# Two transfers instead of one: the spread of the attention's maxima over 125 partitions

## The reference, cut to what matters

```python
scores = jnp.einsum('bhtd,bhsd->bhts', Q, K) * scale
scores = jnp.where(mask, scores, jnp.float32(-jnp.inf))
attn = jax.nn.softmax(scores, axis=-1)
out = jnp.einsum('bhts,bhsd->bhtd', attn, V)
out = out.transpose(0, 2, 1, 3).reshape(B, Tt, D)
out = out @ Wo.T
return hidden_states + jnp.tanh(gate) * out
```

## Time and profile before

| | us |
|---|---|
| median of 3 runs | 1405.7 |
| lowest and highest run | 1401.32, 1408.68 |
| the profiled execution, whole | 1402.65 |
| its span, first to last instruction | 1400.8 |
| PE busy | 1331.3 |
| DVE busy | 928.5 |
| ACT busy | 734.7 |
| POOL busy | 489.8 |

### The profile page before, as it was taken

The page is one execution under the profiler, slowest core; times in us unless marked ns, Lnnn a source line. Parts: engine busy times, 40 slices in busy tenths (PEclk is TensorE's granted clock), DMA queues, the critical chain, the costliest instruction groups (busy, mean ns, idle before and its releaser), DMA issues.

```text
span 1400.8 us, 42823 instructions
## 1 busy us (share of the span) xinstructions
PE 1331.3 (95%) x17120; PEld 937.6 (67%) x17120; DVE 928.5 (66%) x2431; ACT 734.7 (52%) x1772; POOL 489.8 (35%) x550
## 2 busy tenths in 40 slices
PE   6999999999999999897899999999999999999977
PEld 5777777777777777666566666766676667666624
DVE  3555555555555555547677877787888888887862
ACT  4776677767667667632425453445345434444332
POOL 3222111222222222113346445543555345534540
PEclk9999999999999999988999999999999999999979
DMA  7333222222222223113000010001010110010000
GB/s 228 99 106 106 93 75 63 74 73 71 61 76 74 75 69 101 54 57 122 22 21 14 23 28 21 15 22 28 22 27 9 28 27 22 10 26 22 15 14 14
DMA packets 39529, 73.70 MB, mean 53 GB/s; under 512 B 17797, under 2 KB 20485, under 8 KB 37829
## 3 DMA queue, kind: packets, MB, share of 16 engines
q1 hardware_dynamic: 39365, 71.24, 17.2%
HBM read 60.24 MB, written 7.57 MB: 48 GB/s over the span
## 4 chain that ended last, share of the span: by engine, by line
PE 82%; DVE 8%; issue 6%; DMA 2%; ACT 1%; SPq 1%; POOL 0%; DVEq 0%; ACTq 0%; POOLq 0%
PE b_bank L1831 18%; PE b_bank L1837 12%; PE ring_bank L703 7%; PE ring_bank L704 6%; PE ring_bank L705 6%; PE av_bank L789 4%; PE b_bank L1945 4%; PE score_banks L762 4%; DVE probs L450 3%; PE b_bank L1982 3%; PE score_banks L749 3%; PE b_bank L1971 2%; PE b_bank L1885 2%; DVE probsT L467 2%; PE av_bank L775 2%
## 5 line engine op out<-in xcount | busy, mean ns | idle before, releaser
L1126 POOL TENSOR_TENSOR rst<-rp,st 128x448 f32<-128x448 f32 x192 | 209.7, 1115 | 55.9 <-DVE st L1349 53.9
L450 DVE CUSTOM_DVE_ANT_0 probs<-score_banks,unmask 112x375 f32<-112x375 f32 x256 | 124.8, 544 | 93.0 <-issue 93.0
L595 ACT ACTIVATE probs<-probs,least_inv 112x375 f32<-112x375 f32 x256 | 152.4, 606 | 32.5 <-DVE least_inv L450 32.5
L467 DVE SCALAR_TENSOR_TENSOR probsT<-score_banks,least_cols 125x448 f32<-125x448 f32 x192 | 107.9, 617 | 53.9 <-PE score_banks L762 51.7
L610 ACT ACTIVATE probsT<-probsT,key_mask 125x448 f32<-125x448 f32 x192 | 114.5, 661 | 47.4 <-DVE probsT L467 47.2
L1118 POOL TENSOR_TENSOR xm<-mixed,xa 128x448 f32<-128x448 f32 x80 | 88.0, 1102 | 145.3 <-DVE mixed L1278 140.0
L340 POOL TENSOR_TENSOR aT_lo<-whole,aT_hi 128x375 fp32r<-128x375 f32 x64 | 59.0, 921 | 152.3 <-ACT whole L576 150.2
L375 POOL TENSOR_TENSOR ctx_rstd<-ctx_var_eps,a_eps_exp 125x3 f32<-125x3 f32 x16 | 13.8, 865 | 272.6 <-DVE ctx_var_eps L423 272.6
L703 PE MATMUL ring_bank<-aT_hi,wk_lo 128*128 128x376 f32 x256 | 91.2, 356 | 0.2 <-issue 0.2
L1628 ACT COPY key<-b_bank 128x448 f32<-128x448 f32 x16 | 8.5, 533 | 148.4 <-PE b_bank L1831 148.4
L704 PE MATMUL ring_bank<-aT_lo,wk_hi 128*128 128x376 f32 x256 | 85.5, 334 | 0.0
(11 more groups left out here) (183 smaller groups left out, 3109.0 us busy)
## 6 DMA issues: line engine op xcount, KB each, us to landing
least_cols<-values_of_two_batches SPq DMA_DIRECT2D x32, 437.5 KB
ctx_tok<-in_ctx SPq DMA_DIRECT2D x16, 672.0 KB
xT_sb<-in_xT SPq DMA_DIRECT2D x16, 224.0 KB, 2.9
inv_cols<-values_of_two_batches SPq DMA_DIRECT2D x128, 28.0 KB, 3.9
x_tok<-in_x SPq DMA_DIRECT2D x16, 224.0 KB, 2.7
x_between_layers<-x_tok SPq DMA_DIRECT2D x16, 224.0 KB, 4.7
b_x<-x_between_layers SPq DMA_DIRECT2D x16, 224.0 KB, 3.0
x_post<-x_between_layers SPq DMA_DIRECT2D x16, 224.0 KB, 2.9
```

Source lines behind the costliest of these rows:

```text
L450: dve.tensor_tensor_reduce(out=probs[:, g % 2, i], in0=score_bank[0:T, i, 0:TC], in1=unmask[:, m[1]], scale=-SCALE, scalar=-LOWEST, op0=AL ...
L467: dve.scalar_tensor_tensor(out=probsT[:, g % 2, k].rearrange("p (i t) -> p i t", t=T), in0=score_bank[0:TK, :, k * T:(k + 1) * T], scalar= ...
L595: act.activation(probs[:, g % 2, i], probs[:, g % 2, i], ACT.Exp, scale=-1.0, bias=least_at(m, g, i), accum_out=sums[:, g, i:i + 1]).then_ ...
L1126: pool.tensor_tensor(by_chunk(rst[:, j % NPROD]), by_chunk(rp[:].rearrange("p c t -> p (c t)")), state_of(j), ALU.mult).then_inc(s_pprod, 1)
```

## The change

The one transfer onto 125 partitions is issued as two, onto partitions 0 to 111 and 112 to 124, each with the same two source rows. Both count on the same semaphore, so the wait asks for 32 where it asked for 16. The order of everything else stays.

```diff
-            sp.dma_start(least_cols[:, 2 * half:2 * half + 2],
-                         rows_in_dram(half, 0).rearrange("(o g) f -> o g f", o=1).broadcast_to([TK, 2, HG * T])).then_inc(s_least_in[half], 16)
+            for part in CTX_PARTS:
+                sp.dma_start(least_cols[part, 2 * half:2 * half + 2],
+                             rows_in_dram(half, 0).rearrange("(o g) f -> o g f", o=1).broadcast_to(
+                                 [part.stop - part.start, 2, HG * T])).then_inc(s_least_in[half], 16)
...
-                dve.wait_ge(s_least_in[g // 2], 16 * count(m, 1, 1))
+                dve.wait_ge(s_least_in[g // 2], 32 * count(m, 1, 1))
```

## The result

| | before | after |
|---|---|---|
| median of 21 runs, us | 1405.03 | 1398.78 |
| lowest run, us | 1399.84 | 1396.83 |
| the profiled execution, us | 1402.65 | 1402.71 |

The ratio of the runs is 0.9965, with a 95% interval from 0.9955 to 0.9975: 4.9 us less (3.5 to 6.3), within 0.5%. Both profiled spans are 1400.8 us. That is not a contradiction: the execution profiled after is the slowest of its 21, and the one before is among the faster of its own. So the two traces must be compared stretch by stretch and not by their ends.

The account below looks back on a forecast made before the run. PE was taken to bound the kernel, busy 1331.3 of 1400.8 us; only the last step's 1.2 us wait would go, with nothing from the loop, giving 1404.5 us off a median of 1405.7; range 1399.5 to 1409.0.

Parts of the forecast that it names:

- The transfer uses about five engines: Spread of the maxima: 125 partitions use about 5 of 16 engines, 112 would use 16; 2.2 of 3.2 us go.
- landing of 3.7 us: Split transfer of the maxima: lands 3.7 us after its first issue instead of 5.56, bounds 2.7 and 6.9 us.
- The second issue: SP's queue: the split's second transfer costs one more step of SP, 0.3 us with the gap behind it.
- Nothing is gained in the loop: Attention's loop: transfers already have 2.8 to 10.6 us of slack, so a batch stays at 36.4 us.
- SP's extra issues are covered: SP: 32 more issues, 9.6 us in all, covered by its 297.3 us of standing in front of line 266.
- The whole stall goes: Last step, half 1: DVE's whole wait of 1.21 us for the maxima goes, for any landing under 4.4 us.
- PE takes the gain: Last step: of PE's 1.97 us idle, 1.21 go and pass through fully to the store; 0.76 us of idling stay.
- A: Rival, last step: the clock stays up behind the shorter idle time, 1.6 us more, -2.8 us, 1402.9 us; chance 0.17.
- D: Rival, loop: lighter DMA traffic also removes PE's gaps, 4.6 us, 5.8 with the last step, 1399.9 us; chance 0.07.
- B: Rival, the split transfer: 112 partitions spread no better, the wait grows by 0.3 to 1.3 us, 1406.0 to 1407.0; chance 0.10.
- C: Rival, second layer: the moved timing brings lower-clock stretches of 1.6 us each, slower; chance 0.06.
- the sign that the prediction set for it: Profile after: the prediction is wrong if stretches at the lower clock come or go by more than two.

Follow-up runs that it names:

- e3: Against the kernel before, the maxima's transfer stays one but goes onto 128 partitions instead of 125; ratio 0.9978, median 1399.55 us.
- the two filled: The kernel before with 14 or 7 matmuls added in PE's idle time of the last step, slow transfer kept; ratios 1.0017 and 0.9999.
- e1: Against the kernel before, only the attention's last spread (last batch, half 1) is split, the other 31 stay one transfer; ratio 0.9980, median 1399.49 us.
- f1: The changed kernel, unedited, run again beside fresh runs of the kernel before; ratio 0.9982, median 1400.05 us.
- g2: The changed kernel, unedited, run a third time against the kernel before; ratio 0.9987, median 1402.48 us.
- f2: The kernel before, unchanged, run as if it were a changed one against itself; ratio 1.0021, median 1404.49 us.

## Why the prediction was right, point by point

- **The transfer uses about five engines, and the 112 partitions would spread over all.** Shown: in the same half microsecond the share went from 0.49 to 0.95 and the rate from 149 to 351 GB/s. A landing of 3.7 us was forecast for the split; it has no landing row. The single transfer of e3 has 3.7, but by the prediction's own terms it should have had 5.56 - 2.2 = 3.4, without the second issue. So the same number is partly luck: the spread saved 1.9 us, not 2.2. The second issue was sized at 0.3 us and costs SP 0.49 (0.76 us for two, 0.27 for one), which stayed hidden too. The rule of the Trainium skill on how many engines carry a transfer ("DMA: Bandwidth & Descriptors", "Why a DMA increments its semaphore by 16 and not by 1") holds here for 125, 112 and 128 partitions. Its rule against splitting ("Rules for kernel authors") is given for two halves that each spread over all 16 engines already; the 125 partitions did not, and there the split gained. e3 fits its advice to use one transfer of 128.
- **Nothing is gained in the loop, and SP's extra issues are covered.** Shown: 36.40 us a batch as before, and 543.1 us over 30 spreads with and without the split.
- **The whole stall goes, and PE takes the gain.** Shown: the wait has no row, and DVE's use comes 6.40 us after the write of line 266 instead of 7.69, 1.3 us sooner for the 1.2 forecast. In other executions of the kernel before the same wait was 1.4 to 1.8 us, so 1.21 us was the low end of that term.
- **The clock was held to be a rival, A, with a chance of 0.17.** This is where the size was off: the forecast of 1.2 us puts nothing down for the clock. What A describes was in fact a part of the gain in this pair of traces: in three of the five unfilled executions with the unmoved stall the clock fell behind PE's gap, in none of the six without the wait and in neither of the two filled. That a shorter gap keeps the clock up rests on these counts; what makes it fall in one execution and not in the next stays open. The mean step of those five is (22.23 + 22.60 + 20.81 + 22.74 + 20.79) / 5 = 21.8 us; without the wait it is 19.3. So 2.5 us are to be had in that step, of which 1.5 are the stall and 1.0 the clock's mean share, an estimate from only five executions.
- **The size by the runs.** Five comparisons remove the wait and change nothing else of weight. e1, e3, f1 and g2 give 0.9980, 0.9978, 0.9982 and 0.9987, a mean of 1.8 per mille or 2.6 us, which agrees with the step's 2.5; with the first, 0.9965, the mean is 2.2 per mille or 3.0 us. All five are under 1, and all three copies of the kernel before are at 1 or over. So a gain is there, and it is about two and a half times the 1.2 us that were forecast. The first comparison's 4.9 us (at least 3.5 by its interval) lies above even that. What the excess of some 2 us is stays open; the copies show that one kernel can come out 2 to 3 us apart, and no stretch of the profiles shows it.
- **The time was inside the range by its width, not by its terms.** The ratio on the 1405.7 us from which the forecast started gives 1400.8 us, against 1404.5 forecast and a lower bound of 1399.5; the median of the runs, 1398.78, is below that bound. The bound was set for the gain in the loop, D, which did not come.
- **B and D fell, C was not seen.** B by the share and the missing wait, D by the unchanged loop. For C and the sign that the prediction set for it: in windows of 2 us the granted clock is below 0.95 in ten separate stretches before and in ten after, eight and nine of them behind the store, and in the fourteen profiles there are six to nine behind it.

## What to carry to other kernels

Look for a large transfer with a DMA share near 5/16 while it is alone: its number of partitions may divide badly. Padding the tile to 128 partitions or splitting off a multiple of 16 took the rate here from about 140 to about 350 GB/s, and the landing from 5.56 to 3.7 us. A missing landing time is a weaker sign, since the part on 112 partitions has none either. That is worth something only where the chain of waits goes through the transfer, which here was 1 of 32. Where a stall of PE goes, look at the granted clock behind it in several executions: here it fell in three of five and cost 1.6 us each time, a part of the gain that a single trace shows whole or not at all.

## What the runs showed that I had not expected

After the store, the second layer took 776.5 us in one execution and 783.4 in another, though its code is the same (before, and e1). This scatter of 7 us is larger than the whole effect, and it cannot be seen in a kernel's own diff. Ahead of the step, the stretch between the last two writes of line 266 took 16.3 to 18.5 us. There the scatter is the granted clock: in the kernel before it was below its upper level in the windows from 588 to 600 and the stretch took 17.8 us, in its copy f2 from 592 to 598 and 16.4 us. Everything in front of that, from the first write of line 266 on, took 543.1 us each time. The step between two events close to the edit came out at 19.31 or 19.32 us in all six profiles without the wait and at 20.8 or more in all with it, where 12 runs against 35 left an interval of 3 to 5 us.
